# Two attention layers on one core: half of the first pass's pair tiles moved beside the statistics

## What is computed

```python
# layer 0, on a group norm of x over 32 groups of 8 columns (the last axis)
mu, var = mean and variance of pair_rep over everything
x = (pair_rep - mu) * rsqrt(var + EPS) * ln_w + ln_b
q, k, v = proj(wq), proj(wk), proj(wv);  g = sigmoid(proj(wg_w) + wg_b)
bias = jnp.einsum('hc,bcij->bhij', wb, x)
scores = jnp.einsum('bhcij,bhcik->bhijk', q, k) * scale + bias[:, :, None, :, :]
# layer 1, on a group norm of layer 0's result
bias = jnp.einsum('nijz,zh->nhij', pair_repr, bias_proj)[:, None]
sim = softmax(q k * scale) + bias
```

## Time and profile before

| what | us |
|---|---|
| median of 3 runs (5018.1 to 5019.6) | 5018.24 |
| the profiled execution's own time | 5019.72 |
| its span | 5017.9 |
| TensorE busy | 4723.5 |
| VectorE busy | 4034.1 |
| ScalarE busy | 3555.3 |
| GpSimd busy | 3462.1 |

### The profile page before, as it was taken

How to read it: one execution, slowest core, us unless ns; L and a number is a source line. 1 busy time by engine, 2 the same in 40 slices (tenths; PEclk the granted TensorE clock), 3 DMA queues, 4 the chain that set the end, 5 groups by cost and what they waited for, 6 DMA issues and landing times. The chain is left out here.

```text
span 5017.9 us, 150143 instructions
## 1 busy us (share of the span) xinstructions
PE 4723.5 (94%) x44087; PEld 3884.7 (77%) x44087; DVE 4034.1 (80%) x12779; ACT 3555.3 (71%) x11216; POOL 3462.1 (69%) x5926
## 2 busy tenths in 40 slices
PE   4663999999999999999999969999999999999999
PEld 2332888888888888888888858888888888888887
DVE  4445888888888888888888878888888888888887
ACT  2222888888888888888888846666666666666665
POOL 2333888888888888888888836666666666666665
PEclk8776999999999999999999979999999999999999
DMA  8994111111111111111111101111111111111111
GB/s 330 357 353 156 52 59 50 59 50 59 50 59 50 59 51 58 53 56 56 53 58 50 58 29 39 50 50 50 50 50 50 50 50 50 50 50 50 50 51 43
DMA packets 237329, 382.52 MB, mean 76 GB/s; under 512 B 18756, under 2 KB 156616, under 8 KB 224968
## 3 DMA queue, kind: packets, MB, share of 16 engines
q1 hardware_dynamic: 237256, 381.63, 22.7%
HBM read 309.21 MB, written 72.35 MB: 76 GB/s over the span
## 5 line engine op out<-in xcount | busy, mean ns | idle before, releaser
L1301 POOL TENSOR_SCALAR l_probs<-l_probs,l_inv 128x256 f32<-128x256 f32 x2048 | 943.6, 478 | 738.4 <-DVE l_inv L1206 732.8
L1125 ACT ACTIVATE l_probs<-bank,l_neg_max 128x256 f32<-128x256 f32 x2048 | 948.9, 482 | 487.0 <-DVE l_neg_max L1200 487.0
L544 POOL TENSOR_SCALAR l_probs<-l_probs,l_inv 128x256 f32<-128x256 f32 x2048 | 975.0, 489 | 414.0 <-DVE l_inv L796 414.0
L715 ACT ACTIVATE l_probs<-l_probs,l_neg_max 128x256 f32<-128x256 f32 x2048 | 1011.4, 504 | 0.8 <-DVE l_neg_max L788 0.8
L788 DVE CUSTOM_DVE_ANT_0 l_probs<-bank,bias 128x256 f32<-128x256 f32 x2048 | 746.9, 421 | 275.5 <-PE bank L657 204.1
L1200 DVE TENSOR_REDUCE l_neg_max<-bank 128x2 f32<-128x512 f32 x1024 | 647.1, 684 | 93.4 <-PE bank L1034 93.4
L1213 DVE TENSOR_TENSOR l_probs_t<-bank,bias 128x512 f32<-128x512 f32 x1024 | 674.7, 683 | 36.7 <-PE bank L1044 17.3
L657 PE MATMUL bank<-ident,l_probs 128*128 128x128 f32 x4096 | 601.1, 279 | 1.4 <-POOL l_probs L544 1.1
L669 PE MATMUL bank<-l_probs_t,l_v 128*64 128x256 f32 x4096 | 555.0, 392 | 1.5 <-DVE l_probs_t L810 0.9
L657 PEld LDWEIGHTS bank<-ident,l_probs 128*128 128x128 f32 x4096 | 442.6, 141 | 135.3 <-issue 98.3
L1044 PE MATMUL bank<-ident,l_probs 128*128 128x128 f32 x4096 | 531.7, 273 | 3.4 <-DVE l_probs_t L1213 1.7
(11 more groups left out here) (193 smaller groups left out, 14057.4 us busy)
## 6 DMA issues: line engine op xcount, KB each, us to landing
fp_x<-in_x_dram SPq DMA_DIRECT2D x32, 1024.0 KB, 6.9
fp_ln_w<-in_L_conv_ln_w_dram SPq DMA_DIRECT2D x32, 1024.0 KB, 8.9
fp_ln_b<-in_L_conv_ln_b_dram SPq DMA_DIRECT2D x32, 1024.0 KB, 10.2
fp_pair<-in_L_conv_pair_repr_dram SPq DMA_DIRECT2D x32, 1024.0 KB, 12.0
l_x<-in_x_dram SPq DMA_DIRECT2D x128, 256.0 KB, 2.9
l_ln_w<-in_L_conv_ln_w_dram SPq DMA_DIRECT2D x128, 256.0 KB, 3.4
l_ln_b<-in_L_conv_ln_b_dram SPq DMA_DIRECT2D x128, 256.0 KB, 3.5
x<-l_y SPq DMA_DIRECT2D x128, 256.0 KB, 2.0
```

Of the source, the lines that this page charges most:

```text
L544: last = nc.gpsimd.tensor_scalar(probs[:, h, c], probs[:, h, c], inv[:, h, c:c + 1], 1.0, ALU.mult, ALU.mult)
L715: last = nc.scalar.activation(probs[:, h, c], probs[:, h, c], ACT.Exp, bias=neg_max[:, h, c:c + 1], scale=-1.0, accum_out=total[:, h, c:c ...
L1125: last = nc.scalar.activation(probs[:, h, c], b_s[h % 4][:, c * W:(c + 1) * W], ACT.Exp, bias=neg_max[:, h, c:c + 1], accum_out=total[:, h ...
L1301: last = nc.gpsimd.tensor_scalar(probs[:, h, c], probs[:, h, c], inv[:, h, c:c + 1], 1.0, ALU.mult, ALU.mult)
```

## The change

In the first pass a period is now four image tiles and two pair tiles. Pair tiles 0 to 15 go with the image tiles, one behind every second of them; pair tiles 16 to 31 follow in the same block when the last image tile is through ("late pairs"). All four strips of a turned pair tile are copied by ScalarE. The pair tile has its own evacuation buffer, its own stores and its own semaphores.

VectorE's work on the image is written out without a loop: after each four tiles 32 `bn_aggr` make one piece (count 1, mean, variance) of each group from the last 24 values, and the last aggregation takes the 8 pieces, 24 values, of each group.

The statistics of layer 0 have no block of their own any more: a class `Statistics` holds their steps, and they are called inside the first pass, TensorE's two matmuls after late pairs 20 and 21, ScalarE's roots after late pairs 22 and 23. The bias parts are loaded once the image stores have landed, ahead of the late pairs' loads. Layer 1's bias is loaded at the start of the second statistics. The sums and products of both layers are the same.

```diff
+            def image_tile(tile, t, i):
+                pe.wait_ge(loaded[i], 48 * (t + 1))
+                wait(pe, evacuated, tile)
+                project(b_part[W_PART], m.wb_t[:], wt[i]).then_inc(projected[W_PART], 1)
+                project(b_part[B_PART], m.wb_t[:], bt[i]).then_inc(projected[B_PART], 1)
+                pe.wait_ge(weighted, tile + 1)
+                project(b_part[X_PART], m.wb_t[:], xt[i]).then_inc(projected[X_PART], 1)
+            def pair_tile(tile, t, i):
+                pe.wait_ge(pair_loaded[i], 16 * (t + 1))
+                for j in range(STRIPS):
+                    wait(pe, copied, STRIPS * (tile - 1) + j + 1)
+                    for r in range(2):
+                        for e in range(2):
+                            last = nc.tensor.transpose(b_turned[j][:, (2 * r + e) * P:(2 * r + e + 1) * P], raw[i][:, 2 * j + r, e, :], m.ident[:])
+                    last.then_inc(transposed, 1)
+                pe.wait_ge(copied, STRIPS * (tile + 1))
+                wait(pe, pair_evacuated, tile)
+                project(b_pair, m.w_pair[:], turned[i]).then_inc(pair_projected, 1)
+            over_tiles(pe, image_tile, pair_tile)
+            pe.wait_ge(evacuated, TILES)
+            for tile in late_pairs:
+                pair_tile(tile, tile // 2, tile % 2)
+                if tile == late_pairs[4]:
+                    statistics.tensor(pe, 0)
+                if tile == late_pairs[5]:
+                    statistics.tensor(pe, 1)
...
+                for k in range(PERIOD):
+                    if not (last and k >= PERIOD - 2):
+                        load_image(PERIOD * t + k + 2, k % 2)
+                    store_image(PERIOD * t + k, k % 2)
+                    if k % 2:
+                        load_pair(2 * t + k // 2 + 2, k // 2)
+                        store_pair(2 * t + k // 2, k // 2)
...
+            for part, to in ((W_PART, bias_w), (X_PART, m.bias0), (B_PART, bias_b)):
+                for a in range(KC):
+                    sp.dma_start(to[:, a], image_parts[part, :, a * P:(a + 1) * P, :].rearrange("h p k -> p h k")).then_inc(parts_loaded, 16)
+            for tile in late_pairs:
+                if tile + 2 < TILES:
+                    load_pair(tile + 2, tile % 2)
+                store_pair(tile, tile % 2)
...
+                dve.wait_ge(measured, PERIOD * (t + 1))
+                dve.wait_ge(counted, 1)
+                for g in range(NG):
+                    last = nc.vector.bn_aggr(pieces[:, g, t, 1:3], stats[:, g, 0:PERIOD, :])
+                last.then_inc(piece_ready, 1)
+            dve.wait_ge(piece_ready, TILES // PERIOD)
+            dve.wait_ge(evacuated, TILES)
+            chain = statistics.vector(dve, lambda g: pieces[:, g], True)
...
+            for tile in late_pairs:
+                pair_tile(tile, tile // 2, tile % 2)
+                if tile == late_pairs[6]:
+                    statistics.scalar(act, 0)
+                if tile == late_pairs[7]:
+                    statistics.scalar(act, 1)
...
-        finish_statistics(nc, m, "gs0", stats, lambda g: W // 8, True, (image_parts, pair_bias))
         layer0(nc, m, x, ln_w, ln_b, x1, stats)
-
-        finish_statistics(nc, m, "gs1", stats, lambda g: W // 8 + (g < NG - 4), False, turn_bias=True)
+        finish_statistics(nc, m, stats, lambda g: W // 8 + (g < NG - 4), pair_bias)
```

More of the change, by code:

```diff
@@ L230, in first_pass @@
         turned = sb("pair_t", [P, ROWS, W])
[L231 to L236, removed]
+        evac = sb("evac", [P, 3, 2 * W])
@@ new lines, in _, with project @@
+        @block.tensor
+        def _(pe):
+            def project(bank, weights, rows):
+                for c in range(STRIPS):
+                    last = nc.tensor.matmul(bank[32 * c:32 * c + 32, :], weights, rows[:, 2 * c:2 * c + 2, :].rearrange("p r k -> p (r k)"),
+                                            start=True, stop=True, tile_position=(0, 32 * c))
+                return last
+            def image_tile(tile, t, i):
[24 more added lines that the diff above has]
+                    statistics.tensor(pe, 1)
@@ L240, in _ @@
         def _(sp):
[L241 to L245, removed]
-                for part in (X_PART, W_PART, B_PART):
-                    wait(sp, projected[part], tile - 1)
-                image.load(sp, tile, i)
[L249 to L257, removed]
@@ L259, in _ @@
-            load_pair(0, 0)
-            load_pair(1, 1)
[L262 to L267, removed]
-            for i in range(2):
-                sp.wait_ge(stored[i], 16 * STORES * TILES // 2)
+            for a in range(KC):
+                sp.dma_start(m.bias1[:, a], pair_bias[:, a * P:(a + 1) * P, :].rearrange("h p k -> p h k")).then_inc(pair_loaded, 16)
@@ L271, in _ @@
+        @block.vector
+        def _(dve):
+            statistics.vector(dve, lambda g: stats[:, g, 0:chunks(g), :], False)
+        @block.scalar
+        def _(act):
+            for h in range(NH1):
+                act.wait_ge(bias_mm, h + 1)
+                nc.scalar.activation(m.bias1[:, :, h], b_bias[h % 6][:].rearrange("p (a c) -> p a c", a=KC), ACT.Copy).then_inc(bias_out, 1)
+            statistics.scalar(act, 0)
         @block.tensor
         def _(pe):
-            def project(part, tile, weights, rows):
-                wait(pe, evacuated, tile)
-                for c in range(PAIRS):
-                    last = nc.tensor.matmul(m.psum[part][32 * c:32 * c + 32, :], weights, rows[:, 2 * c:2 * c + 2, :].rearrange("p r k -> p (r k)"),
-                                            start=True, stop=True, tile_position=(0, 32 * c))
-                last.then_inc(projected[part], 1)
@@ L457, in layer0 @@
+            pe.wait_ge(pair_loaded, 16 * KC)
+            for h in range(NH1):
+                wait(pe, bias_out, h - 5)
+                for kc in range(KC):
+                    for qc in range(KC):
+                        last = nc.tensor.transpose(b_bias[h % 6][:, kc * W + qc * P:kc * W + (qc + 1) * P], m.bias1[:, qc, h, kc * P:(kc + 1) * P], m.ident[:])
+                last.then_inc(bias_mm, 1)
+            statistics.tensor(pe, 0)
+            statistics.tensor(pe, 1)
 def layer0(nc, m, x, ln_w, ln_b, x1, stats):
```

313 lines of the change are left out of this document (158 added, 155 removed).

## The result

The changed kernel takes **5004.73 us** (median of 8 runs, 4998.9 to 5014.6), the kernel before 5018.96 us (8 runs, 5017.3 to 5025.1, the three told of ahead of the change among them). The ratio is 0.9971 with a 95% interval of 0.9960 to 0.9982: 14.2 us faster, between 9 and 20. The forecast was 5005.5 us, with faster by over 10 us as the likeliest case. The profiled execution took 5004.06 us, its span is 5002.2 us.

The account below looks back on a forecast made before the run. The first pass is bound by its transfers, DMA busy 0.96 at 354 GB/s. Layer 0's first load 12.8 us sooner takes 5019.7 to 5006.9; the median lies 1.5 lower: 5005.5 us, 8 in 10 from 4989 to 5028.

Parts of the forecast that it names:

- beat, two image tiles and a pair tile: First pass: transfers set the period, 21.2 us for two image tiles against 24.56 before, upper end 22.5 us.
- pair tile 18: Late tiles: its load stands behind the bias parts in SP's queue and lands at X + 23; TensorE stalls 7.5 us.
- a late tile at full clock: Late pair tiles on TensorE, one after the other: copies, hand-over and projection take 4.2 to 4.4 us, taken as 4.3.
- sum: Up to layer 0's first load: 466.8 us before, 454 after, 12.8 us less.
- term of 8.65 us for an image tile's loads: Part of the pass's beat: 3 MiB of image loads, what the old beat leaves after pair loads and stores.
- The pass's mean rate, 21.5 us: First pass: alternative price of two tiles, 7.60 MB at 354 GB/s, named but not taken.
- rival 3: First pass: transfer and buffer loops rub, 22 us or more per two tiles, 5016 to 5023 us; chance 0.13.
- SP added no wait: First pass: stores behind a pair load, only every second tile and 4 instead of 8, delay no image load.
- The start: Start of the pass: image tile 0 goes first on TensorE, done at 34.4 us; tile 3 lands at 53 us.
- The clock: Late tiles: TensorE starts at 0.5, rises during tile 16, and stays high since no gap exceeds 1.5 us.
- Rival 1: Late tiles 19 to 31 at low clock: 6.3 instead of 4.3 us each, 25 us more, 5030 us; chance 0.17.
- the 28 us become 4 + 4: VectorE's aggregation in the old tail shrinks from 28 us to 4 + 4, hidden beside the late pair tiles.

Follow-up runs that it names:

- Experiment 3: Changed kernel with GpSimd's product of x and ln_w left out of the first pass, projection waiting for the statistics alone: 4986.11 us, ratio 0.9931.
- experiment 6: Changed kernel with late tiles pipelined: transposes of tile n+1 ahead of tile n's projection, ScalarE's copies ahead of the evacuation; 5031.64 us, ratio 1.0024.
- experiment 1: Kernel before with the partial aggregation alone added: 4999.0 us, ratio 0.9957.
- experiment 2: Changed kernel without the partial aggregation, the last aggregation taking all 192 values: 5000.52 us, ratio 0.9962.
- experiment 11: Kernel before with the partial aggregation and layer 1's bias loaded at the second statistics, pair tiles not moved: 4998.55 us, ratio 0.9957.
- experiment 7: Changed kernel with four raw buffers for the late tiles, pair loads 18 and 19 ahead of the bias parts: 5007.73 us, ratio 0.9977.
- experiment 9: Changed kernel with late tiles pipelined and SP issuing the stores of tile n-1 behind the load of tile n+2: 4999.74 us, ratio 0.9961.
- experiment 8: Changed kernel with bias parts spread one by one, four raw buffers and late tiles pipelined, all together: 4994.17 us, ratio 0.9948.
- experiment 5: Changed kernel with the six bias part loads one by one behind the stores of every second late tile: 5001.45 us, ratio 0.9964.

## Why the prediction was right

| step | predicted | measured |
|---|---|---|
| image tile 3 | 53 us | 54.65 |
| beat, two image tiles and a pair tile | 21.2 us | (356.95 - 54.65) / 14 = 21.59 |
| image tile 31 | 350 us | 356.95 |
| end of the last image projection, X | 360 us | 366.8 |
| one partial aggregation | 0.13 us | 4.04 / 32 = 0.126 |
| pair tile 18 | X + 23, stall 7.5 | X + 22.9, stall 9.78 |
| a late tile at full clock | 4.3 us | 4.0 |
| layer 0's first load | X + 94 = 454 us | X + 89.1 = 455.87 |
| sum | 12.8 us less | 10.95 in the profile, 14.2 by the medians |

*The pass.* The mechanism was right and the beat was 0.39 us too short, 5.5 us over fourteen periods. Its term of 8.65 us for an image tile's loads is what the old beat leaves, while 3 MiB at the 423 GB/s named beside it are 7.4; the prediction has nothing for the 1.2 us between them. The pass's mean rate, 21.5 us, which the prediction names and doesn't take, would have been nearer. Experiment 3 adds that the release of the buffers has a small share in it (0.5 us), a mild form of rival 3. SP added no wait, as said: its stores behind a pair load end at 206.02 us in the middle of the pass, and the image tile is released at 205.96. The start was 1.65 us later than worked out; 1.0 of it is that VectorE's first statistics begin at 25.51 us, behind a memset of 0.70 us for the pieces, and not at 24.52. One piece wasn't priced: with no pair tile ahead of it, TensorE comes to many image projections of x at the low clock (1.93 us instead of 1.03; the mean matmul takes 938 ns between 60 and 356 us, and took 594 before), so some tiles are released 0.9 us later.

*The late tiles.* The regular tile is 0.3 us shorter than the sum of its hand-overs. ScalarE's table load and the low clock behind it cost some 3 us, as allowed for: the projection at 417.32 us waits 2.42 us instead of 1.0, and the transposes after it take 3.63 us instead of 1.97. Pair tile 18 came at X + 22.9 by the transfers' working; the stall is longer because tiles 16 and 17 were done sooner. *The clock* held: 0.95 from 396 to 452 us, where the low level shows right behind the gap and once behind ScalarE's table load. Rival 1 did not happen here: in the regular late tiles TensorE pauses 1.0 us ahead of each projection, and the transposes behind stay at 1.97 us. The Trainium skill (TensorE: Matmul & The Clock Gate, "A second HAM failure mode: psum-queue depth-cycling") tells of a kernel in which brief, frequent pauses between groups of matmuls make the clock go back and forth; this trace does not agree for pauses of 1.0 us. In experiment 6 the clock does go back and forth, but behind waits of 3.9 to 5.1 us for a load, which are another case than brief pauses.

*The statistics.* Hidden as said. VectorE ends at 430.3 us, some 25 us ahead of layer 0's first load. But the prediction said only that the 28 us become 4 + 4, and didn't ask what each half of the change is worth by itself. Experiments 1 and 2 did: 18 to 19 us each by the medians, 14 together. The halves are rivals for one gap. That is the step that the prediction leaves out: its total came out without it. What the move costs on top is the late tiles' chain: 17 tiles, one after the other, and a stall behind the parts.

*Errors that cancelled.* The pass was 7 us late, the late tiles 5 us early. By the profile alone the gain is 10.95 us up to layer 0, against 12.8 in the sum, and by experiment 11 what the spans differ by beyond that is scatter; the medians' interval of 9 to 20 us holds either. The near agreement of 5004.73 with 5005.5 us is in part luck, better than the terms are.

*Layer 1's bias.* It landed, TensorE turned it from 2948.27 us in 5.05 us, and then waited 15.79 us for VectorE: the 14 us of slack that were worked out.

```profile
2969.11 0.69 PE L282 MATMUL bank<-gs_own,averager 128*128 128x64 f32 x2 [15.79 <-DVE gs_own L236]
```

Experiment 11 confirms the price of nothing.

## What to carry to other kernels

Before work is moved to cover a gap, look for what can shrink the gap where it stands: 28 us of aggregation went to 4 with a few lines in the pass, and covering them with other work then brought nothing more. In a queue that issues in a fixed order, a store that waits for a later event holds every load behind it; when a pipeline is deepened, move the stores behind the next load as well, or the queue undoes the gain. Where a chain and a buffer loop have nearly the same length, shortening one alone gains little (experiments 7 and 9); with both shortened, look for the next limit, which was the transfers in experiment 8.

## What the runs showed that was not expected

- Waits of the same length can lie on either side of the clock. Behind ScalarE's table load TensorE waits 2.42 us in the changed kernel, and the transposes that follow take 3.63 us, the low clock; in experiments 2 and 7 it waits 2.43 us at the same place, and they take 1.97. Ahead of the transposes, a wait of 1.90 us was followed by 2.40 us of them (experiment 6), one of 2.13 us by 2.81 and one of 2.06 us by 1.97 (both experiment 5). Behind the longer waits, of 3.8 us and more, they took 2.4 to 3.7 us each time. What decides between the two isn't shown.
- SP can need three times as long to issue the same small stores. Four stores of 16 KB took 1.30 us at 372.53 us, ahead of the 3 MiB of parts, and 3.94 us at 380.35 us, right behind the parts and a pair load. The parts' last two issues took 2.83 us, the first two 0.95.
- From the second statistics to the end, where no experiment changes more than the place of one load, single executions differ by up to 6 us (2062.2 to 2068.2). Of two profiles of this kernel, differences in one stage are to be trusted sooner than differences of the whole span.
